# Six restoring additions on the count matrix, moved from VectorE to GpSimd

## What is computed

```python
def conv(h, W, b):
    h = h @ W
    agg = jax.ops.segment_sum(h[src] * norm, dst, num_segments=n)
    return agg + b
h = jax.nn.relu(conv(x, W1, b1))
h = jax.nn.relu(conv(h, W2, b2))
return conv(h, W3, b3)
```

## Time and profile before

| | |
|---|---|
| median of 3 runs | 869.26 us (867.94 to 869.59) |
| the profiled execution, its own time | 868.13 us |
| its span in the profile | 864.0 us |
| PE busy | 823.6 us (95%) |
| DVE busy | 606.2 us (70%) |
| ACT busy | 297.5 us (34%) |
| POOL busy | 117.0 us (14%), the last of it at 441.7 us |

### The profile page before, as it was taken

One profiled execution on the slowest core, in us unless ns is written; L12 is line 12 of the kernel. 1 busy time (PEld: TensorE's weight loads), 2 busy tenths in 40 slices (PEclk: granted clock), 3 DMA queues, 4 the chain that ended last, 5 costly groups with the idle time before them and its releaser, 6 DMA issues.

```text
span 864.0 us, 14285 instructions
## 1 busy us (share of the span) xinstructions
PE 823.6 (95%) x4710; PEld 466.9 (54%) x4710; DVE 606.2 (70%) x1319; ACT 297.5 (34%) x604; POOL 117.0 (14%) x244
## 2 busy tenths in 40 slices
PE   2889999999999996999999999999999999999997
PEld 1357566666666444455545545555554555455554
DVE  8945999999999277253869546575664746565677
ACT  3365666776766222110101212221302122112233
POOL 0210110012000046555730000000000000000000
PEclk9889999999999998999999999999999999999999
DMA  6100000000000512332111112222705112111232
GB/s 205 33 2 1 4 18 23 17 17 17 24 17 17 172 38 76 111 75 75 40 35 55 53 55 85 74 86 79 214 3 163 32 42 51 31 36 42 57 79 53
DMA packets 83769, 49.83 MB, mean 58 GB/s; under 512 B 46667, under 2 KB 80220, under 8 KB 83692
## 3 DMA queue, kind: packets, MB, share of 16 engines
q1 hardware_dynamic: 73836, 39.00, 16.1%
q10 hardware_dynamic: 9856, 9.85, 3.6%
HBM read 29.68 MB, written 18.78 MB: 56 GB/s over the span
## 4 chain that ended last, share of the span: by engine, by line
PE 83%; DVE 11%; issue 2%; DMA 2%; ACT 1%; SPq 1%; ACTq 0%; DVEq 0%
PE ps L1396 16%; PE ps L1058 13%; PE ps L1743 9%; PE ps L1570 8%; PE ps L955 8%; PE ps L757 5%; PE ps L764 5%; PE ps L1421 5%; PE ps L1439 3%; PE ps L769 2%; PE ps L774 2%; PE ps L1030 2%; DVE node_b L298 1%; DVE count L598 1%; PE ps L986 1%
## 5 line engine op out<-in xcount | busy, mean ns | idle before, releaser
L1058 PE MATMUL ps<-node_a,count 128*128 128x512 f16 x525 | 181.1, 381 | 1.5 <-DVE node_a L1165 1.0
L955 PE MATMUL ps<-node_b 128*128 128x175 f16 x808 | 162.3, 256 | 6.7 <-DVE node_b L298 5.3
L298 DVE TENSOR_TENSOR node_b<-node_b 128x1024 f16<-128x1024 f16 (+2 forms) x253 | 157.3, 670 | 0.0
L1254 ACT ACTIVATE count<-ps 128x500 f32 x202 | 122.8, 608 | 65.2 <-PE ps L955 59.5
L1396 PE MATMUL ps<-count,node_a 128*128 128x512 f16 (+2 forms) x686 | 130.7, 351 | 0.0
L955 PEld LDWEIGHTS ps<-node_b 128*128 128x128 f16 x808 | 79.5, 100 | 36.0 <-issue 6.2
L2327 POOL TENSOR_TENSOR count<-count,node_a 16x20 f16 x202 | 86.1, 426 | 92.8 <-DMA chapter_starts<-in_dst 52.3
L1396 PEld LDWEIGHTS ps<-count,node_a 128*128 128x128 f16 (+1 forms) x686 | 60.1, 98 | 69.1 <-issue 0.4
L1743 PE MATMUL ps<-count,node_a 128*128 128x512 f16 x288 | 64.1, 379 | 0.0
L1058 PEld LDWEIGHTS ps<-node_a,count 128*128 128x128 f16 x525 | 53.2, 101 | 18.9 <-ACT count L1254 1.2
L1701 DVE TENSOR_TENSOR count<-count 128x6144 f16<-128x6144 f16 x14 | 46.9, 3353 | 17.6 <-PE ps L1570 16.3
(11 more groups left out here) (289 smaller groups left out, 1137.2 us busy)
## 6 DMA issues: line engine op xcount, KB each, us to landing
node_a<-second_scratch ACTq DMA_DIRECT2D x6, 768.0 KB, 4.3
node_a<-in_x SPq DMA_DIRECT2D x4, 768.0 KB, 8.4
second_scratch<-node_a ACTq DMA_DIRECT2D x4, 768.0 KB, 3.5
state_scratch<-params SPq DMA_DIRECT2D x24, 128.0 KB, 1.9
node_b<-state_scratch SPq DMA_DIRECT2D x96, 32.0 KB, 2.1
table_scratch<-agg SPq DMA_DIRECT2D x21, 128.0 KB, 1.8
mixed_scratch<-node_b SPq DMA_DIRECT2D x10, 256.0 KB, 2.0
node_a<-mixed_scratch SPq DMA_DIRECT2D x4, 640.0 KB, 6.8
```

Of the source, the lines that this page charges most:

```text
L298: return DVE.tensor_tensor(to, iota, keys.unsqueeze(2).to_broadcast([P, n, width, 2]), ALU.is_equal)
L955: return PE.matmul(window(s)[:, :, keys], low, key_hot[k][:, j, :, i].rearrange("p (t w) -> p t w", w=SPAN), start=(s == 0 and j == 0), st ...
L1058: last = PE.matmul(out_slot(u)[0:m, :], count[:, t, u * P:u * P + m], node_a[:, t, :, :].rearrange("p a d -> p (a d)"), start=(t == 0), st ...
L1254: ACTE.activation(to, window(s), ACT.Copy).then_inc(win_written, 1)
```

## The change

The six restoring additions leave DVE's list. GpSimd makes them, behind its last small block, in the order y, a12, a21 of pair 1 and then of pair 2, each waiting for the one before it by a semaphore of their own, `restored`. PE waits for that semaphore ahead of chunks 2 to 5 of layer 3, and DVE waits for it ahead of taking off the self loops of these chunks. The eight other steps of the two pairs stay on DVE, and the numbers of the semaphore `step_made` are renumbered.

```diff
@@ layers_pe, layer 3, ahead of chunks 2 to 5
                 if c // 2 in PAIRS_OUT:
-                    PE.wait_ge(*second_step_at("a21" if c % 2 else "a12", c // 2))
+                    PE.wait_ge(*restored_at("a21" if c % 2 else "a12", c // 2))
@@
-        SECOND_STEPS = [("s1", 1), ("s1", 2), ("s2", 1), ("s4", 1), ("s3", 1), ("s2", 2), ("s4", 2), ("y", 1), ("a12", 1), ("a21", 1),
-                        ("s3", 2), ("y", 2), ("a12", 2), ("a21", 2)]
+        SECOND_STEPS = [("s1", 1), ("s1", 2), ("s2", 1), ("s4", 1), ("s3", 1), ("s2", 2), ("s4", 2), ("s3", 2)]
+        RESTORED = ("y", "a12", "a21")
@@
+        def restored_at(which, p):
+            return restored, 3 * (p - 1) + RESTORED.index(which) + 1
+
+        def restore_pool(p):
+            a11, y, x, a22 = block(p, 0, 0), block(p, 0, 1), block(p, 1, 0), block(p, 1, 1)
+            POOL.wait_ge(rel_rows_free, 1)
+            if p > 1:
+                POOL.wait_ge(*restored_at("a21", p - 1))
+            POOL.wait_ge(*second_product_at(p, T3))
+            POOL.tensor_tensor(y, y, x, ALU.add).then_inc(restored, 1)
+            POOL.wait_ge(*restored_at("y", p))
+            POOL.tensor_tensor(y, y, a22, ALU.add).then_inc(restored, 1)
+            POOL.wait_ge(*restored_at("a12", p))
+            POOL.tensor_tensor(x, x, a11, ALU.add).then_inc(restored, 1)
@@ layers_dve, pair 2
                 second_step_dve("s4", p)
-                if p == 2:
-                    second_step_dve("y", 1)
                 second_add_dve(p, "c11")
-                if p == 2:
-                    second_step_dve("a12", 1)
-                    second_step_dve("a21", 1)
                 second_add_dve(p, "c12")
                 second_step_dve("s3", p)
@@ layers_dve, behind layer 2
             DVE.memset(node_b[:, T - 1, :, :], 0.0).then_inc(rel_cleared, 1)
-            second_step_dve("y", 2)
...
-            second_step_dve("a12", 2)
-            second_step_dve("a21", 2)
@@ loops_dve
             DVE.wait_ge(sums_done, H_THIRD + HALVES * (i + 1))
+            if c // 2 in PAIRS_OUT:
+                DVE.wait_ge(*restored_at("a21", c // 2))
@@ end of fast_pool
             POOL.memset(node_a[rel_rows, T - 1, 0, :], 0.0).then_inc(rel_rows_free, 1)
+            for p in PAIRS_OUT:
+                restore_pool(p)
```

More of the change, by code:

```diff
@@ L839, in program @@
         rel_cleared, rel_again, rel_high, rel_table = (sem(n) for n in ("rel_cleared", "rel_again", "rel_high", "rel_table"))
-        parts_low = sem("parts_low")
+        parts_low, restored = sem("parts_low"), sem("restored")
         x1_added, norm_ready, x1_shaped = sem("x1_added"), sem("norm_ready"), sem("x1_shaped")
@@ L1689, in second_step_dve @@
             a11, y, x, a22 = block(p, 0, 0), block(p, 0, 1), block(p, 1, 0), block(p, 1, 1)
-            to, of, op = {"s1": (x, a22, ALU.add), "s2": (x, a11, ALU.subtract), "s4": (y, x, ALU.subtract), "s3": (x, a22, ALU.subtract),
-                          "y": (y, x, ALU.add), "a12": (y, a22, ALU.add), "a21": (x, a11, ALU.add)}[which]
+            to, of, op = {"s1": (x, a22, ALU.add), "s2": (x, a11, ALU.subtract), "s4": (y, x, ALU.subtract), "s3": (x, a22, ALU.subtract)}[which]
             n = SECOND_STEPS.index((which, p))
@@ L1725, in step_at @@
         def step_at(p, which):
-            return step_made, 14 + 3 * p + STEPS.index(which) + 1
+            return step_made, 8 + 3 * p + STEPS.index(which) + 1
         def bank_of(p, which):
```

## The result

The changed kernel takes 915.94 us (median of 4 runs, 914.64 to 917.87) against 868.6 us in the runs of before that go with it: ratio 1.055, 95% interval 1.0521 to 1.0579. It is 47.3 us slower; the forecast was 907.3 us in a range of 874 to 935.

What follows compares the result with a forecast made beforehand. PE was taken to bound the kernel, with nothing to gain. 0.9 + 35.1 for the hold + 2 for the clock = 38 us on 868.13 gives 906.1; the median, 1.13 above, makes 907.3, range 874 to 935.

Steps and rivals of the forecast that it cites:

- The price of a step: One GpSimd addition over 6144 numbers: 0.2 us fixed and about 1.9 ns a number, 12.0 us.
- A long GpSimd instruction holds DVE for its whole length: A two-input DVE instruction from SBUF meeting a GpSimd step waits until it ends, up to 12.0 us each time.
- The first rival: A long GpSimd instruction lets DVE in between, so L1919 loses only tenths of a us; time stays at 869; 12%.
- nor is L1925 at 375.00, in which a whole POOL addition lies: In the trace before, L1925 and a POOL addition of 0.22 us both keep their length, so L1925 is not held.
- The second rival: L1925 is held too, so chunk 4's last tile waits for the end of a21(2): loss 44 us, time 915; 8%.
- One tile per step: In chunk 4, POOL's next step enters after each L1919, and the next tile's L1919 waits some 12 us for it.
- The forecast signs: POOL's steps 0.4 to 3.5 us apart; five L1919 stretched to 4 to 12 us; L1925 stays at 0.35.
- What PE waits for: PE waits on L1919's line between 456 and 514 us, 35 us in all, for tiles of chunks 4 and 5.
- The walk: POOL's and DVE's lists followed from 428 us: POOL ends at 509.9, PE is 36.0 us late at chunk 0.
- the term for the hold: PE's lateness when chunk 0 is summed, at 516.4 instead of 480.4: 36.0 us, the first 0.9 included.
- slower steps: Rival: GpSimd's steps cost towards 3.3 ns a number; at 16.2 us a step 932, at 20.4 us 957; 6% beyond 932.
- PE's clock: After PE's waits, the sums from 510 us on may run at a lower clock: 2 us, bounds 0 and 5.

Runs made afterwards that it cites:

- e1: The kernel before with the six restoring additions left out altogether, on DVE and on POOL: 867.42 us, ratio 0.9992.
- e10: The changed kernel with GpSimd multiplying the same blocks by 1.0 in place of the six additions, plus a wait that was already met: 929.53 us, one execution.
- e5: The changed kernel with each of GpSimd's six steps cut into twelve instructions of one tile, each waiting for the one before: 877.14 us, ratio 1.0096.
- e8: The changed kernel with GpSimd filling the same blocks with zeros in place of the six additions, plus a wait that was already met: 879.27 us, one execution.
- e9: The changed kernel with only y and a12 of pair 1 on GpSimd; DVE makes a21 of pair 1 and all of pair 2: 870.61 us, ratio 1.0038.
- e7: The changed kernel with PE making the products of chunk 5 behind the 20th SOON tile of f = 0, not the fourth: 914.64 us, ratio 1.0539.
- e4: The changed kernel with one more wait, so POOL begins its six whole steps only when all tiles of layer 2 are ready: 914.26 us, ratio 1.0531.

## Why the prediction was right, and where its steps were off

- **PE bounds, and there is nothing to gain.** Right, and shown by e1.
- **The price of a step**, 12.0 us from the rows of 20 and of 128 numbers: measured 11.8. The two-size fit over a 48 times larger block held. Its slope was taken a little high: (424 - 220) / 108 is 1.89 ns a number and not 1.92, and with it the fit gives 11.8. The estimate from the Trainium skill's figure (GPSIMD Engine Reference, section 3.1), 13.5 us, was 1.7 too high for this type and shape.
- **A long GpSimd instruction holds DVE for its whole length.** Right for the additions: 11.50 us for an L1933 of 0.42. Beside a one-input multiplication L1933 is let go 1.4 us before the end (e10). The first rival is out. e5, e8 and e9 show that it is the hold that costs, and not deadlines (no wait on the restored blocks) or GpSimd's amount of work.
- **POOL's start and s3.** 432.5 forecast, 431.1 measured, which is 432.6 with the 1.5 us by which this execution is ahead; s3 to end at 447.85, measured 446.1 (447.6); PE to be 0.9 us late at T3, measured 446.20 (447.7), 0.7 late.
- **"nor is L1925 at 375.00, in which a whole POOL addition lies"** is the step that failed. I took from it that L1925 is never held. It is: 4.51, 11.86 and 11.85 us in the changed kernel, and 4.48 by a fill. The row could not show it, and it was misread: POOL's 0.22 us began 0.23 us into an instruction of 0.35, so the two overlap for 0.12 us and the addition ends 0.10 us behind L1925. Rows of the same trace spoke for the rival. Here, in the kernel before, POOL's addition begins 0.10 us into an L1925, meets no other instruction of DVE, and takes 0.33 us where it takes 0.22 by itself, to 0.09 us behind L1925's end:

```profile
355.64 0.34 DVE L1925 TENSOR_SCALAR pair_a<-pair_a,dscale 53x256 f32<-53x256 f32 x1
355.74 0.33 POOL L2327 TENSOR_TENSOR count<-count,node_a 16x20 f16 x1 [0.21 <-POOL count L2327]
```

  The addition of 375.23 ends 0.10 us behind its L1925, as this held one does, so that row says nothing either way. The second rival, a rule of the Trainium skill (SBUF — State Buffer, Who interferes with whom), had the mechanism and gave 915 us, next to the 915.9 measured, though not by the right walk: it got 8% of the chances, and the nearness of its number is luck.
- **"One tile per step".** It was two steps a tile. POOL gets its turn directly behind L1933, ahead of L1939, and so both are held. The forecast signs fail with it: POOL's steps stand 0.1 us apart and not 0.4 to 3.5, and two L1933 and three L1939 are stretched, where five L1933 were to be and no L1939.
- **What PE waits for.** I had PE waiting at the end of f = 0's SOON, with the sixteen tiles before it done in the holes and f = 1's 8.7 us as well. PE stood instead in the products of chunk 5, for a PSUM bank that L1929 had to read, with all of chunk 0 but four tiles still to do. The walk named L1919's line for 35 us; the profile names L1929's for 45.1. These two steps together made the term for the hold too small: forecast 36.0, measured 47.8 - 1.9 = 45.9 us behind chunk 0 by position (the 1.9 is the clock, below), and 47.4 from the mark. That POOL was done at 505.3 and not at 509.9 took back part of it. In e7's trace the place of the wait is worth 3.1 us; with long steps DVE sets most of it wherever PE stands.
- **The sum.** With the step and the clock as measured, the walk gives 868.13 + 36.0 - 1.2 + 1.9 + 1.13 = 906 us. That 915.9 lies in the range is owed to the width that was kept for slower steps, and these did not come.
- **PE's clock**, forecast 2 us. PE's windows after:

```profile
485.00:505.00 20.00, 0.00 (x0) 0.50 0.00 0
505.00:512.00 7.00, 6.11 (x20) 0.68 0.14 41
512.00:530.00 18.00, 18.00 (x128) 1.00 0.10 30
```

  and the last tile's products before:

```profile
459.96 0.59 PE L1421 MATMUL ps<-params,xt 128*128 128x256 f32 x2
```

  The granted clock is 0.50 (1.2 GHz) through the wait and 0.68 on average in the next 7 us. From the start of the last tile's four matmuls to chunk 0's row it is 507.75 - 505.89 = 1.9 us, and in the kernel before, at 2.4 GHz, 460.82 - 459.96 = 0.9; chunk 0's row is 21.71 for 20.83. That is 1.9 us in all.
- **The rest moves as a whole.** Right, 47.8 us by position at 529 and at 644.

## What to carry to other kernels

An engine that is idle is not free if its instructions and those of a busy one keep each other out: here a long GpSimd instruction turned a 0.4 us VectorE instruction into a 12 us one. Before moving work there, list VectorE's instructions beside it that have two SBUF inputs (like L1933) or are a tensor_scalar from SBUF to SBUF (like L1939), and follow who waits for what stands behind them, through the other engines too (e4). If the move must be, put it where VectorE reads PSUM (e9: two steps for 2.8 us), or cut it into pieces (e5: 9 us for 47). And ask first, with a kernel that leaves the work out, whether there is anything to gain.

## What the runs showed of the hardware that I had not expected

- GpSimd's one-input multiplication of 6144 float16 numbers takes 15.72 us, longer than the two-input addition of the same block (11.8); a fill takes 5.22 to 5.24.
- L1933 was let go 1.4 us before that multiplication ended, L1939 only at the end (e10).
- GpSimd got its turn between two VectorE instructions that follow each other without a gap (469.76 in the changed kernel, with L1933 ending at 469.90 and L1939 issued at 469.83). What decides the turn stays open; no run was made for it.
